# Wide attention scores as two full-height passes in place of three half-height ones

## What is computed

```python
x = x + jnp.tanh(g_xattn[2]) * _L2_xattn_ref(_layernorm(x, axis=-1), ctx_768, L2_xattn_w_q, L2_xattn_w_k, L2_xattn_w_v, L2_xattn_w_o, L2_xattn_b_o)
```

## Time and profile before

| what | value |
|---|---|
| median of 3 runs | 2401.87 us (2387.91 to 2403.25) |
| the profiled run: its time | 2405.62 us |
| the profiled run: its span | 2403.9 us |
| busy PE / PEld / DVE / ACT / POOL | 82% / 64% / 55% / 32% / 33% |
| mean granted TensorE clock | 0.868 of full speed |

### The profile page before, as it was taken

How to read it: one execution, slowest core, us unless ns; L and a number is a source line. 1 busy time by engine, 2 the same in 40 slices (tenths; PEclk the granted TensorE clock), 3 DMA queues, 4 the chain that set the end, 5 groups by cost and what they waited for, 6 DMA issues and landing times.

```text
span 2403.9 us, 33562 instructions
## 1 busy us (share of the span) xinstructions
PE 1970.7 (82%) x12232; PEld 1529.6 (64%) x12232; DVE 1316.6 (55%) x2824; ACT 769.3 (32%) x1697; POOL 782.9 (33%) x694
## 2 busy tenths in 40 slices
PE   3589699942999999869999999599967888448997
PEld 2467566532777777757778787478855555336664
DVE  2434478551555444345555555565546898446773
ACT  1122146400222121134444444122322445112554
POOL 4110101054355444256666555454533200100000
PEclk9789679655999999879999999599985889776898
DMA  4280456123333332220000001034626542023341
GB/s 142 84 279 0 58 77 88 22 81 116 110 110 119 110 110 92 82 68 16 13 13 13 4 1 66 3 105 136 205 78 112 86 66 29 0 36 56 57 74 41
DMA packets 120190, 177.88 MB, mean 74 GB/s; under 512 B 10916, under 2 KB 105188, under 8 KB 117412
## 3 DMA queue, kind: packets, MB, share of 16 engines
q1 hardware_dynamic: 91092, 128.36, 23.4%
q0 software_dynamic: 8448, 26.52, 3.7%
q10 hardware_dynamic: 20496, 20.97, 2.6%
HBM read 89.26 MB, written 47.19 MB: 57 GB/s over the span
## 4 chain that ended last, share of the span: by engine, by line
PE 59%; issue 12%; DVE 11%; POOL 9%; DMA 5%; ACT 2%; SPq 1%; DVEq 0%; POOLq 0%; ACTq 0%
PE bank L1846 13%; PE bank L1847 10%; PE bank L1848 10%; PE bank L2125 5%; PE bank L2157 4%; POOL ewl L785 3%; DMA ew<-in_we 3%; PE bank L2005 3%; PE bank L2020 3%; PE bank L1979 2%; DVE nmf L1144 2%; PE bank L2142 1%; POOL ewh L783 1%; POOL rows_by_expert L797 1%; PE bank L2167 1%
## 5 line engine op out<-in xcount | busy, mean ns | idle before, releaser
L1144 DVE TENSOR_REDUCE nmf<-bank 128x2 f32<-128x512 f32 x384 | 260.8, 689 | 120.4 <-PE bank L2125 117.6
L1719 ACT ACTIVATE pT<-bank 128x512 f32<-128x512 f32 x384 | 224.8, 597 | 249.6 <-PE bank L2142 247.6
L1407 DVE TENSOR_TENSOR bank<-sil,bank 128x512 f32<-128x512 f32 x136 | 94.8, 697 | 285.0 <-ACT sil L1774 284.5
L2125 PE MATMUL bank<-kpack,qpack 48*128 48x256 f32 (+1 forms) x768 | 202.1, 370 | 53.6 <-DVE nmf L1144 30.9
L1846 PE MATMUL bank<-split,ewl 128*128 128x512 f32 x514 | 212.1, 413 | 24.2 <-POOL ewl L785 13.9
L1847 PE MATMUL bank<-split,ewh 128*128 128x512 f32 (+1 forms) x578 | 228.7, 396 | 0.0
L1848 PE MATMUL bank<-split,ewh 128*128 128x512 f32 (+1 forms) x578 | 227.7, 394 | 0.0
L2125 PEld LDWEIGHTS bank<-kpack,qpack 48*128 48x128 f32 (+1 forms) x768 | 128.6, 222 | 134.8 <-DVE nmf L1144 63.9
L785 POOL TENSOR_TENSOR ewl<-ew,ewh 128x1536 fp32r<-128x1536 f32 (+1 forms) x47 | 205.9, 4380 | 3.8
L2142 PE MATMUL bank<-qpack,kpack 50*128 50x256 f32 (+1 forms) x768 | 198.5, 359 | 9.2 <-ACT pT L1719 9.1
L783 POOL CAST ewh<-ew 128x1536 fp32r<-128x1536 f32 (+1 forms) x47 | 85.2, 1813 | 325.0 <-DMA ew<-in_we 314.3
(11 more groups left out here) (431 smaller groups left out, 4757.7 us busy)
## 6 DMA issues: line engine op xcount, KB each, us to landing
ew<-in_we SPq DMA_DIRECT2D x32, 768.0 KB, 7.8
ew<-in_we SPq DMA_DIRECT2D x15, 1408.0 KB, 6.2
rows_by_expert<-zeros ACTq DMA_DIRECT2D x1, 20480.0 KB, 62.5
kpack<-khl SPq DMA_DIRECT2D x144, 128.0 KB, 4.0
qpack<-qhl SPq DMA_DIRECT2D x144, 128.0 KB
arena<-rows_by_expert SPq DMA_DIRECT2D x23, 512.0 KB, 4.2
rows_by_expert<-arena SPq DMA_DIRECT2D x38, 256.0 KB, 5.5
ct<-in_ctxT SPq DMA_DIRECT2D x32, 192.0 KB, 2.4
```

Source lines behind the costliest of these rows:

```text
L1144: V.tensor_reduce(nmf[:, c, :, j, r], bank[s.banks[i % len(s.banks)]][:, :] .rearrange("p (t k) -> p t k", t=T), AXX, ALU.max, negate=True ...
L1719: A(pT16[i % 8][:, :], bank[2 + h % 2][:, :], ACT.Exp, scale=s.qscale).then_inc(m["e"], 1)
L2125: ins = mm(bank[s.banks[i % len(s.banks)]][:, t * S:(t + 1) * S], q[rows, r, t * P:(t + 1) * P], k[rows, r, :], start=True, stop=True)
```

## The change

A head's scores become two passes of 128 rows. One operand stacks the head's queries: the high part in its own 64 partitions, the low part in the other 64. The other operand is, in the first pass, the high keys in both halves; in the second the low keys in the own half beside zeros. The sum over both passes is the same three products as before. `keys2` so has an entry for each of the two heads (e) and twice the size; `queries2` has a block for each head, and of its three buffers the second and half of the third lie in a new tile, `rows3`, in the memory of `raw3`. Therefore the loading of `raw3` moves to POOL's list in the second mixture (layer l2f), with a semaphore of its own, w4_in. DVE writes the six blocks of zeros once, ahead of its loop.

```diff
-        raw3 = sb("raw3", [P, 3, DC, D])
+        raw3 = under("raw3", [P, 3, DC, D])
+        rows3 = sb("rows3", [P, 3 * DC * D], F32R)
...
-        keys2 = [t.rearrange("p (w g s) -> p w g s", w=2, g=2) for t in threes(0, 4 * S)]
-        queries2 = [t.rearrange("p (w g s) -> p w g s", w=2, g=2) for t in threes(3072, 4 * S)]
+        keys2 = [t.rearrange("p (e w g s) -> p e w g s", e=2, w=2, g=2) for t in threes(0, 8 * S)]
+        queries2 = [[t[:, o + e * 512:o + e * 512 + 512].rearrange("p (g s) -> p g s", g=2) for e in range(2)]
+                    for t, o in ((split, 6144), (rows3, 0))]
+        queries2.append([t[:, o:o + 512].rearrange("p (g s) -> p g s", g=2) for t, o in ((split, 7168), (rows3, 1024))])
...
-            loads += [(raw3[:, 0, :, :], a["wq_l3f"]), (raw3[:, 1, :, :], a["wk_l3f"]), (raw3[:, 2, :, :], a["wv_l3f"])]
+            later3 = [(raw3[:, 0, :, :], a["wq_l3f"]), (raw3[:, 1, :, :], a["wk_l3f"]), (raw3[:, 2, :, :], a["wv_l3f"])]
...
                     for dst, src in later:
                         pool.dma_start(dst, src).then_inc(g["w3_in"], 16)
+                    for dst, src in later3:
+                        pool.dma_start(dst, src).then_inc(g["w4_in"], 16)
...
+                    pool.wait_ge(g["w4_in"], 16 * 3)
                     split_packed(L3F)
...
-                    tt(keys2[u % 3][:, 1, :, :], src, keys2[u % 3][:, 0, :, :], ALU.subtract).then_inc(done, 1)
+                    for e in range(2):
+                        own = slice(64 * e, 64 * e + 64)
+                        ins = tt(keys2[u % 3][own, e, 1, :, :], src[own, :, :], keys2[u % 3][own, e, 0, :, :], ALU.subtract)
+                    ins.then_inc(done, 1)
...
-                    stt(queries2[u % 3][:, 1, :, :], src, s.qscale, queries2[u % 3][:, 0, :, :], ALU.mult, ALU.subtract)\
-                        .then_inc(done, 1)
+                    for e in range(2):
+                        own, other, to = slice(64 * e, 64 * e + 64), slice(64 - 64 * e, 128 - 64 * e), queries2[u % 3][e]
+                        ins = stt(to[other, :, :], src[own, :, :], s.qscale, to[own, :, :], ALU.mult, ALU.subtract)
+                    ins.then_inc(done, 1)
...
+                for u in range(3):
+                    for e in range(2):
+                        other = slice(64 - 64 * e, 128 - 64 * e)
+                        V.tensor_copy(keys2[u][other, e, 1, :, :], zeros[other, :, :].broadcast_to([64, 2, S]))\
+                            .then_inc(m["kz"], 1)
...
-                    copy(keys2[u % 3][:, 0, :, :], groups(from_)).then_inc(m["kh"], 1)
+                    for e in range(2):
+                        own = slice(64 * e, 64 * e + 64)
+                        copy(keys2[u % 3][64 - 64 * e:128 - 64 * e, e, 0, :, :], groups(from_)[own, :, :])
+                        ins = copy(keys2[u % 3][own, e, 0, :, :], groups(from_)[own, :, :])
+                    ins.then_inc(m["kh"], 1)
...
-                    A(queries2[u % 3][:, 0, :, :], groups(from_), ACT.Copy, scale=s.qscale).then_inc(m["qh"], 1)
+                    for e in range(2):
+                        own = slice(64 * e, 64 * e + 64)
+                        ins = A(queries2[u % 3][e][own, :, :], groups(from_)[own, :, :], ACT.Copy, scale=s.qscale)
+                    ins.then_inc(m["qh"], 1)
...
-                    r = slice(64 * e, 64 * e + 64)
-                    for t in range(T):
-                        ins = mm3(bank[i % 2][:, t * S:(t + 1) * S],
-                                  [queries2[u % 3][r, w, k, t * P:(t + 1) * P] for w in range(2)],
-                                  [keys2[u % 3][r, w, k, :] for w in range(2)], True, True)
+                    for t in range(T):
+                        for w in range(2):
+                            ins = mm(bank[i % 2][:, t * S:(t + 1) * S], queries2[u % 3][e][:, k, t * P:(t + 1) * P],
+                                     keys2[u % 3][:, e, w, k, :], start=w == 0, stop=w == 1)
```

More of the change, by code:

```diff
@@ L436, in xnb @@
             return xn[:, t, :] if b == 0 else on[t][:, :]
-        names = ("x_in", "w0_in", "w0f_in", "att_in", "consts", "tanh", "phase", "out_done", "w3_in", "w2a_in", "w2b_in", "w2c_in",
+        names = ("x_in", "w0_in", "w0f_in", "att_in", "consts", "tanh", "phase", "out_done", "w3_in", "w2a_in", "w2b_in", "w2c_in", "w4_in",
                  "xn", "xnT", "xt", "rq", "rd", "zero", "masked")
@@ L444, in group @@
             return {n: sem(f"{p}_{n}") for n in ns}
-        wx = group("l2x", "ct", "cs", "wh", "wl", "xh", "kh", "qh", "s", "mx", "e", "psum", "pn", "pT", "pTc", "pv", "oc", "dve",
+        wx = group("l2x", "ct", "cs", "wh", "wl", "xh", "kh", "kz", "qh", "s", "mx", "e", "psum", "pn", "pT", "pTc", "pv", "oc", "dve",
                    "mp0", "mp1", "mp2", "mf0", "mf1", "mf2")
@@ L1985, in scores @@
                     u, k, e = i // 4, i // 2 % 2, i % 2
+                    if i == 0:
+                        pe.wait_ge(m["kz"], 6)
                     if i % 4 == 0:
```

## The result

The changed kernel takes 2384.83 us (median of 15 runs, 2378.22 to 2394.43); the kernel before, in 15 runs beside it, 2394.62 us (2387.91 to 2406.71). The ratio is 0.9956, with a 95% interval from 0.9937 to 0.9976: 10 us faster, and about 0.4%, where 32 us were forecast. The time lies inside the range that I gave, 2344 to 2386, but by luck: the kernel before had a median of 2401.87 us when I wrote the range, and 0.9956 of that would be 2391. The profiled run took 2391.04 us with a span of 2389.3.

The account below looks back on a forecast made before the run. PE was taken to bound the stage: -60 us of its work, +13 and +5 of waits, +10 clock, +2 start, -1.6 moved loads, so -32 us. Forecast 2370 us against a median of 2401.87, range 2344 to 2386.

Parts of the forecast that it names:

- The passes and the steps between tiles: On PE, 32 fewer passes and fewer tile changes save 7.5 us a round, 60 us in 8 rounds, bounds 53 and 66.
- The bias addition: Where the old batch ends, PE waits 0.7 us for DVE's bias addition, which frees a bank, 7 times: 5 us.
- The start: Zero blocks hidden on DVE; the first keys' extra copies lie ahead of their bank's next use: 2 us, bounds 0 and 4.
- POOL's first root: Three load issues moved off the chain ahead of a root that DVE waits for: 1.6 us less.
- the steps between tiles did not stay: Rival: the steps are the semaphore wait's price and stay, PE gains 31 us, time about 2381; chance 0.13.
- the copies into the other half: Rival: ACT's crossing key copies are slow; at 3.0 us each the time is 2447; chance 0.05.
- So PE waits 8.7 - 6.85 = 1.8 us, in 7 rounds: 13 us.: Where a round begins, PE waits at the weighted sum for the copy of turned probabilities, which stands behind `combine`.
- After, I put it at +0.4: Start of ACT's first key copy where a round begins, measured from that head's scores; +0.20 before the change.
- each 0.47 apart: ACT's half-height copies start 0.47 us after one another, so four key copies end at +2.4.
- Their second half adds 0.60: The second low-key instruction on DVE, ahead of `combine`, adds 0.60 us.
- The clock: PE's granted clock falls after waits in three of seven rounds, 3.4 us lost each: 10 us, between 0 and 24.
- the third rival: Every wait of PE costs the clock: four more drops by 3.4 us, 14 us, time 2384; chance 0.12.

Follow-up runs that it names:

- e11: Changed kernel, from the fourth pair on each of the four copying steps one 128-row instruction as before (scores wrong there); ratio 0.9842 to the kernel before.
- e9: Changed kernel, from the fourth pair on without the high and low query instructions of the second head of a pair; ratio 0.9929 to the kernel before.
- e2: Changed kernel with ScalarE's four half-height key copies replaced by two of 128 rows, crossing copies left out; ratio 0.9866 to the kernel before.
- e3: Changed kernel without the two crossing key copies of a pair, from the fourth pair on; ratio 0.9882 to the kernel before.
- e6: Changed kernel with the two crossing key copies of a pair made by DMAs on SyncE's queue, nothing left out; ratio 0.9893 to the kernel before.
- e10: Changed kernel, from the fourth pair on without VectorE's second half-height instruction in low keys and low queries; ratio 0.9855 to the kernel before.
- e1: Kernel before with scores of two half-height passes, low queries by high keys left out, no copy added; ratio 0.9927 to the kernel before.

## Why the prediction was wrong

**What held.** The passes and the steps between tiles: 7.5 us a round forecast, 7.55 shown (56.26 - 48.71 in e11), and rows of both steps at 0.12 us. The 0.19 and 0.08 us that I took for a drain are gone with the half-height tiles. The bias addition: 0.7 forecast, 0.6 measured, six times. The start: from the last normalisation of x to the first maximum 12.9 us before, 16.0 after, so +3.1 where I had +2, bounds 0 and 4. POOL's first root comes at 24.23 in place of 26.44, 2.2 us sooner, forecast 1.6. Of the rivals, the steps between tiles did not stay, and the copies into the other half are not slow: 0.60 us, like those that stay in theirs (but the first of them gives up the overlap with the copy ahead of it, 0.62 us in place of 0.48).

**The step that failed: "So PE waits 8.7 - 6.85 = 1.8 us, in 7 rounds: 13 us."** The place and the mechanism were right, the size was not: 4.27 us in five rounds, 3.89 in one, and 5.26 us in the first, at the scores there: 30.5 us in the row of PE's weights, 28.9 in PE's own. By the steps of the forecast:

- "After, I put it at +0.4": measured +1.78. This was the largest error, 1.38 us, and the one without a row behind it. I took ACT as free when PE arrives, because ACT has 25 us of work in a round of 56. But ACT and DVE wait for each other at every pair of keys or queries: high copies, low parts, maximum, exponent, next high copies. I followed that chain through one head and let the heads before it stand as they were; the second query instructions stand in it too. e9 gives them 1.20 us.
- "each 0.47 apart": measured 0.60, so 2.40 us for four and low keys at +4.27 (+2.5 forecast), another 0.39 us. Rows 4 and 5 were read for the duration, which is the same at both heights; the distance was taken from copies of 128 rows that start at partition 0, and between copies that change halves it is not the same.
- "Their second half adds 0.60": the two low-key instructions hold DVE for 1.42 us where one takes 0.60 (1218.94 to 1220.36 against the earlier trace rows), so it adds 0.82. With `combine` and what follows, the copy ended at +10.90 where I had +8.7.
- PE was ready at +6.69, forecast +6.85.

A term that the sum lacks: I read PE's waits before as "1.6 us once and 0.7 us once", but the same view has a third line, which the earlier trace rows doesn't show:

```profile
PE bank L2020 <- ACT w L1545: 1.5, 2, 1.1
```

It is the weighted sum near the end of the stage, waiting for ACT. After, these waits are 3.2 and 1.1 us (line 2045 for ACT's line 1562 above), and at the first heads PE waits 1.3 us more.

**The clock** was forecast at three drops of 3.4 us lost, 10 us. There were eight stretches at half speed in the stage, 34.1 us against 6.8, so up to 13.7 us lost. The sum was near, its parts were not: a stretch in a round lasts 3.4 us (one 6.8) and costs half of it, but each of the six waits of about 4 us had one. That is the third rival's "every wait", at half the price. The runs with waits of 2.2 to 2.4 us (e2, e3, e6) show one behind 5 of 18 such waits, e9 with 3.08 us behind 3 of 6, e10 and e11 with 1.3 and 0.8 us behind none. So a shorter wait would have been worth more than itself.

Together, the windows of the whole stage (the first to the last maximum), before and after:

```profile
1061.40:1496.50 435.10, 431.40 (x2897) 344.33 (x2896) 244.76 (x431) 197.15 (x635) 258.74 (x293) 0.99 0.06 19
1056.30:1478.90 422.60, 383.78 (x2637) 320.13 (x2635) 293.43 (x491) 265.31 (x754) 255.15 (x293) 0.96 0.06 19
```

PE is idle for 3.7 us before and 38.8 after: +35.1, where the sum had 13 + 5. Of the busy time half of the stretches at half speed is the clock's, 3.4 us before and 17.1 after: +13.7. What is left, 428.0 and 366.7 us, is the work: -61.3. That gives -12.5 us, the 12.5 us by which the stage is shorter. Outside it the profiled runs differ by -2.1 us: the last normalisation of x comes 8.2 us sooner, less the 3.1 us of the start, and 3.0 us are lost behind the stage. The clock is at half speed for 300.4 us ahead of the stage in place of 320.9, and for 320.1 behind it in place of 306.7, which is large enough for both; why was not traced. In most experiments too the median fell by less than the stage, by up to 11 us (e11); that part was not traced either.

## What to carry to other kernels

When work is taken from the engine that bounds a stage, the next limit is not the busy time of the others but the longest chain in which they wait for one another; follow it over several steps back, through every instruction that the change adds, and not from the moment at which the bounding engine arrives. Split an instruction by partitions only after counting starts: two halves cost two whole ones, and a little more where they alternate between the halves of the partitions. And spread what is new: the same change with `combine` one head further and the copies moved to a DMA queue gained 1.9% in place of 0.4%.

## What the runs showed of the hardware

**Instructions that change halves don't overlap.** On ACT two copies of 128x512 start 0.47 to 0.49 us apart, with a duration of 0.59 to 0.60. The four key copies of a pair, of which each reads or writes in the other half than the one before it, start 0.60 us apart, and the first of them, which writes from partition 64 on, 0.62 us after a 128-row one. The height alone doesn't do it: in e9 the one query copy that is left reads and writes from partition 0 on, and the exponent behind it starts 0.47 us after it, where it starts 0.62 us after the second query copy of the changed kernel:

```profile
1249.04 0.58 ACT L1625 ACTIVATE rows<-bank 64x512 fp32r<-64x512 f32 x1
1249.51 0.46 ACT L1646 ACTIVATE w<-bank,nmax 128x256 f32<-128x256 f32 x1
```

DVE does the same: its two low-key instructions start 0.70 us apart, and `combine` starts 0.72 us after the second; in e10, where only the one from partition 0 is left, `combine` starts 0.60 us after it (1152.36 and 1152.96), as after a 128-row one. No kernel ran with the copies in an order with fewer changes of half. The Trainium skill, ScalarE: Activation LUTs, What ACT_TABLE_LOAD costs, says that back-to-back instructions overlap by about 93 ns; where the half stays the traces show 0.10 to 0.12 us, where it changes none.

**DVE and POOL stop each other.** The durations of `combine`'s instructions from 1100 to 1400 us (minimum, median, maximum in ns), of the changed kernel and of e10:

```profile
L950 DVE SCALAR_TENSOR_TENSOR x<-w,gw_l1f,x x24: 478/484/1304, 1110.1 to 1389.2; 128x256 f32<-128x256 f32 x24
```

```profile
L950 DVE SCALAR_TENSOR_TENSOR x<-w,gw_l1f,x x24: 466/473/485, 1103.1 to 1354.0; 128x256 f32<-128x256 f32 x24
```

Where POOL's division begins inside `combine`, an instruction of DVE takes 1.30 us in place of 0.48 (1.19 in the kernel before); in e10 POOL is the one that comes second, its instructions take the 0.99 and 1.18 us above, and none of DVE's is longer. The Trainium skill, SBUF — State Buffer, SBUF: two separate sides, has the rule: a VectorE instruction with two operands in SBUF and a GpSimd instruction that reads SBUF exclude each other for a whole instruction. `combine` reads two such tiles, and the rows of both divisions agree. Not every meeting shows it: before, a short POOL instruction of line 837 ran 0.69 us from 1229.78 on, beside `combine`, and neither was longer.

**The clock after a pause.** Behind PE's six waits of about 4 us the clock was at 1.2 GHz for 3.4 us five times and for 6.8 us once. Behind one of 1.6 us in e1 it was there for 20.5 us, with PE's row busy in all of the windows from 1452 to 1460 above. Behind the waits of 1.3 us in e10 and 0.8 us in e11 it stayed at 2.4 GHz in all rounds, and so it did behind the pause of 1.1 us near the end of the stage in the kernel before.
